# Long cross attention: a fourth PSUM bank for the maxima, and the jobs beside the loop in the banks of the scores

## The reference, cut to what matters

```
q = x @ Wq            # (8, 100, 16 heads, 8)
k = context @ Wk      # (8, 1444, 4 heads, 8)
v = context @ Wv
s = q . k / sqrt(8)   # each query head against its group's key head
a = softmax(s over the 1444 keys)
x = x + (a @ v) @ Wo
```

## Time and profile before

| | |
|---|---|
| median of three runs | 1079.68 us |
| the profiled execution | 1077.89 us, span 1076.1 us |
| loop of maxima | 811.7 to 1037.6 us |
| one full pass (six in a row alike) | 28.65 us |
| busy in such a pass | PE 26.8, DVE 25.7, ACT 22.2, POOL 4.1 us |
| granted TensorE clock in it | 1.00 |

### The profile page before, as it was taken

One profiled execution on the slowest core, in us unless ns is written; L12 is line 12 of the kernel. 1 busy time (PEld: TensorE's weight loads), 2 busy tenths in 40 slices (PEclk: granted clock), 3 DMA queues, 4 the chain that ended last, 5 costly groups with the idle time before them and its releaser, 6 DMA issues. The chain is left out here.

```text
span 1076.1 us, 18489 instructions
## 1 busy us (share of the span) xinstructions
PE 894.8 (83%) x6288; PEld 549.2 (51%) x6294; DVE 740.2 (69%) x2034; ACT 583.9 (54%) x1772; POOL 243.5 (23%) x357
## 2 busy tenths in 40 slices
PE   6998999999798273499669799795768999999997
PEld 3346999999465131345443486482752233333333
DVE  7568778777575599376777555514558888988953
ACT  5785777777433100243535344641443777777784
POOL 5004455555200122133030000351401111111110
PEclk9699999999999586599888899996885999999999
DMA  9600000000002700100001002550202001111000
GB/s 232 160 22 1 2 2 2 1 2 2 1 1 35 88 0 2 29 2 1 1 25 32 1 1 71 171 147 16 53 16 63 20 12 24 28 28 21 2 1 16
DMA packets 76185, 35.83 MB, mean 33 GB/s; under 512 B 35236, under 2 KB 74571, under 8 KB 76092
## 3 DMA queue, kind: packets, MB, share of 16 engines
q1 hardware_dynamic: 73724, 33.61, 14.0%
q0 software_dynamic: 896, 0.63, 0.2%
q10 hardware_dynamic: 1472, 0.41, 0.2%
HBM read 24.42 MB, written 11.05 MB: 33 GB/s over the span
## 5 line engine op out<-in xcount | busy, mean ns | idle before, releaser
L503 DVE TENSOR_REDUCE L3x_NMP<-L3x_pM 128x1 f32<-128x361 f32 x384 | 178.2, 525 | 19.9 <-PE L3x_pM L736 19.1
L657 ACT ACTIVATE L3x_E<-L3x_pS 128x400 f32<-128x400 f32 (+1 forms) x375 | 164.5, 509 | 47.2 <-PE L3x_pS L760 46.1
L736 PE MATMUL L3x_pM<-ctx_tm 64*128 64x361 bf16 x384 | 103.7, 340 | 13.9 <-DVE L3x_NMP L503 9.5
L760 PE MATMUL L3x_pS<-ctx_tm 64*128 64x400 bf16 (+1 forms) x375 | 105.4, 350 | 1.6 <-POOL ctx_tm L447 1.2
L1869 ACT ACTIVATE L0x_E<-L0x_E,ctx_r 128x100 f32<-128x100 f32 x288 | 105.1, 369 | 0.5 <-DVE L0x_E L1749 0.5
L736 PEld LDWEIGHTS L3x_pM<-ctx_tm 64*128 64x128 bf16 x384 | 30.2, 96 | 109.4 <-DVE L3x_NMP L503 90.4
L777 PE MATMUL L3x_pO<-L3x_E,CT 128*32 128x400 f32 (+1 forms) x768 | 85.1, 515 | 0.6 <-ACT L3x_E L657 0.4
L1678 POOL TENSOR_TENSOR L0x_E<-L0x_E,L0x_RZ 128x1200 f32<-128x1200 f32 x24 | 52.6, 2194 | 72.3 <-DVE L0x_RZ L1774 72.3
L1995 PE MATMUL L0x_pU<-ctx_tm,L0x_E 128*100 128x129 f32 x576 | 67.8, 273 | 1.1 <-POOL L0x_E L1678 1.1
L1983 PE MATMUL L0x_pS<-L0x_QS,CT 128*128 128x100 f32 x576 | 68.4, 275 | 0.0
L1983 PEld LDWEIGHTS L0x_pS<-L0x_QS,CT 128*128 128x128 f32 x576 | 66.2, 192 | 0.4 <-ACT L0x_QS L1861 0.4
(11 more groups left out here) (706 smaller groups left out, 2122.3 us busy)
## 6 DMA issues: line engine op xcount, KB each, us to landing
ctx_tm<-in_ctx SPq DMA_DIRECT2D x8, 704.0 KB
ctx_tm<-key_terms SPq DMA_DIRECT2D x16, 270.8 KB, 4.2
key_terms<-ctx_tm SPq DMA_DIRECT2D x42, 90.2 KB
ctx_tm<-in_L_ffn_wi SPq DMA_DIRECT2D x4, 512.0 KB, 8.0
ctx_tm<-in_L_ffn_wo SPq DMA_DIRECT2D x4, 512.0 KB, 8.1
ctx_tm<-query_terms SPq DMA_DIRECT2D x16, 75.0 KB, 3.5
slots_in<-L2a_zeros SPq DMA_DIRECT2D x8, 129.0 KB
L2f_XS<-slots_in SPq DMA_DIRECT2D x4, 258.0 KB, 3.4
```

The source lines that it names most:

```text
L503: nc.vector.tensor_reduce(NMP[:, p, i // NC4, a, i % NC4:i % NC4 + 1], v, AX.X, ALU.max, negate=True).then_inc(s_mr, 1)
L657: nc.scalar.activation(E[0:r, n % EB, :], score_bank(n)[0:r, 0:NG * T], ACT.Exp, scale=SCALE8).then_inc(s_e, 1)
L736: nc.tensor.matmul(pM[:, n % 3, 0:CW], key_rows(QS, a)[:, b, p, 128 * x:128 * x + 128], key_rows(KS, a)[:, b % KB, c, p, :], start=True, s ...
L760: nc.tensor.matmul(score_bank(n)[0:NW[k], 0:NG * T], key_rows(KS, a)[:, b % KB, k % 4, p, 128 * (k // 4):128 * (k // 4) + NW[k]], key_rows ...
```

## The change

`pP` goes, and its bank becomes the fourth of `pM`; product n for the maxima now goes to bank n mod 4 and waits for the reduction four before it. The jobs have no bank of their own any more. A loop that runs when the program is built (`banks_in_turn`) goes through the steps and gives each score product and each job one of the three banks of `pS`, always the one that it counts free first. It counts a score's bank free 1 or 1.4 steps after its step, and a job's after the number of steps in `JOB_READ`. It also notes who held the bank before; TensorE waits for the reader of that holder, with `s_e` if it was a score, with `s_read` if it was a job. From the last unit on two banks of `pM` are used as well, and once the maxima are through (t of 208 and more) the jobs go to the fourth bank of `pM`.

```diff
-        pM = s.ps("pM", [128, 3, 512])
+        pM = s.ps("pM", [128, 4, 512])
         pS = s.ps("pS", [128, 3, 512])
         pO = s.ps("pO", [128, 512])
-        pP = s.ps("pP", [128, 512])
...
-        def score_bank(n):
-            return job_banks[n % 3 if n < MORE else (n - MORE) % 5]
...
+        JOB_READ = {"NT": 1.8, "TM": 4.8, "TURN": 1.8, "PROJ": 1.4}
+        shared = [pS[:, 0, :], pS[:, 1, :], pS[:, 2, :], pM[:, 1, :], pM[:, 2, :]]
+        def banks_in_turn():
+            bank, earlier = {}, {}
+            free, holder = [0.0] * len(shared), [None] * len(shared)
+            def take(item, t, until):
+                usable = 5 if t >= start(NU - 1) else 3
+                i = min(range(usable), key=lambda x: free[x])
+                bank[item], earlier[item] = shared[i], holder[i]
+                free[i], holder[i] = until, item
+            for t in range(LAST + 1):
+                at_step = unit_step(t)
+                if at_step is not None:
+                    for a in range(2):
+                        take(("score", 24 * at_step[0] + 2 * at_step[1] + a), t, t + 1 + 0.4 * a)
+                for job in jobs_at(t):
+                    if t >= DRAIN:
+                        bank[job] = pM[:, 3, :]
+                    else:
+                        take(job, t, t + JOB_READ[job[0]])
+            return bank, earlier
...
+                def bank_read(item):
+                    holder = earlier_in_bank[item]
+                    if holder is not None and holder[0] == "score":
+                        pe.wait_ge(s_e, holder[1] + 1)
+                    elif holder is not None:
+                        pe.wait_ge(s_read, number[holder] + 1)
...
-                    if n >= 3:
-                        pe.wait_ge(s_mr, n - 2)
+                    if n >= 4:
+                        pe.wait_ge(s_mr, n - 3)
...
-                    if n >= 3 and bank_reader(n):
-                        pe.wait_ge(s_e, bank_reader(n))
-                    elif n >= 3:
+                    bank_read(("score", n))
+                    if n >= 24 * (NU - 1):
                         pe.wait_ge(s_mr, 2 * DRAIN)
```

More of the change, by code:

```diff
@@ L250, in attention_long @@
     DRAIN = PER * B
-    MORE = 24 * (NU - 1)
     IT = 4
@@ L307, in attention_long @@
         pT = [pS[:, 2, :], pO]
-        job_banks = [pS[:, i, :] for i in range(3)] + [pM[:, 1, :], pM[:, 2, :]]
-        def score_bank(n):
-            return job_banks[n % 3 if n < MORE else (n - MORE) % 5]
[L313 to L317, removed]
         def start(u):
@@ L362, in attention_long, with score_bank @@
                 number[job] = len(number)
+        JOB_READ = {"NT": 1.8, "TM": 4.8, "TURN": 1.8, "PROJ": 1.4}
[19 more added lines that the diff above has]
+            return bank, earlier
+        bank_of, earlier_in_bank = banks_in_turn()
+        def score_bank(n):
+            return bank_of["score", n]
         def key_rows(ap, a):
@@ L494, in maximum @@
                     dve.wait_ge(s_m, m_count(n + 1))
-                    v = pM[:, n % 3, 0:CW]
+                    v = pM[:, n % 4, 0:CW]
                     if o // 2 in (REM_AT, REM_AT + 1):
@@ L522, in normalised @@
                         dve.wait_ge(s_fill, number["TURN", b - 1] + 1)
+                    pP = bank_of["TM", b]
                     chain.then(nc.vector.reciprocal(rden[:, :], pP[0:T, D:D + NH]))
@@ L530, in residual @@
                     dve.wait_ge(s_fill, number["PROJ", b] + 1)
-                    nc.vector.tensor_tensor(m.X[:, b, :], m.X[:, b, :], pP[0:T, 256:256 + D], ALU.add)\
+                    nc.vector.tensor_tensor(m.X[:, b, :], m.X[:, b, :], bank_of["PROJ", b][0:T, 256:256 + D],
+                                            ALU.add)\
                       .then_inc(s_read, 1)
@@ L669, in maxima @@
                         act.wait_ge(s_add, u - 1)
-                    nc.scalar.copy(NB[:, u % 2, :], pP[:, 0:NG * T]).then_inc(s_read, 1)
+                    nc.scalar.copy(NB[:, u % 2, :], bank_of["NT", u][:, 0:NG * T]).then_inc(s_read, 1)
                 def outT(b):
@@ L675, in outT @@
                         act.wait_ge(s_fill, number["PROJ", b - 1] + 1)
-                    nc.scalar.copy(OT[:, :], pP[:, 144:144 + T]).then_inc(s_read, 1)
+                    nc.scalar.copy(OT[:, :], bank_of["TURN", b][:, 144:144 + T]).then_inc(s_read, 1)
                 for t in range(LAST + 1):
@@ L706, in fill @@
                         pe.wait_ge(s_read, number[job])
+                    if job in earlier_in_bank:
+                        bank_read(job)
+                    else:
+                        pe.wait_ge(s_mr, 2 * DRAIN)
+                    return bank_of[job]
                 for i, (a, e) in enumerate(PARTS):
@@ L729, in max_scores @@
                         for p in range(2):
-                            nc.tensor.matmul(pM[32 * p:32 * p + 32, n % 3, 0:CW], QR[:, p, b, :],
+                            nc.tensor.matmul(pM[32 * p:32 * p + 32, n % 4, 0:CW], QR[:, p, b, :],
                                              KS[:, b % KB, c, p, :], start=True, stop=True,
@@ L740, in turn_maxima @@
                 def turn_maxima(u):
-                    fill(("NT", u))
+                    pP = fill(("NT", u))
                     pe.wait_ge(s_mx, u + 1)
@@ L794, in turn @@
                 def turn(b):
-                    fill(("TURN", b))
+                    pP = fill(("TURN", b))
                     nc.tensor.transpose(pP[:, 144:144 + T], ON[:, :], m.ident[0:T, 0:T]).then_inc(s_fill, 1)
                 def project(b):
-                    fill(("PROJ", b))
+                    pP = fill(("PROJ", b))
                     nc.tensor.matmul(pP[0:T, 256:256 + D], OT[:, :], wo[:, :], start=True, stop=True)\
```

2 lines of the change are left out of this document (1 added, 1 removed).

## The result

The changed kernel is slower. Its median of four runs is 1097.28 us (1093.19 to 1102.62), beside 1079.30 us (1077.50 to 1080.97) for four runs of the kernel before. The ratio is 1.0165, with a 95% interval of 1.0139 to 1.0190. The profiled execution took 1093.19 us, the lowest of the four, with a span of 1091.4 us. The forecast of 1089 us had the sign right and was 8 us short; the result lies 4 us above the forecast's own range (1083 to 1093) and 3 us above the wider one (1076 to 1094).

A forecast was written before the change was run, and what follows sets the result against it. VectorE bounds, sometimes starved by TensorE's late products. Head -2.45, six passes +12.4 and the end +0.2 give some +10.2 on the profiled 1077.89, 1088.1, or 1089.9 by median; forecast 1089, range 1083 to 1093, wider 1076 to 1094.

The forecast's parts named there:

- The walk: Event-by-event count through pass 3 with unit costs, each engine in written order: pass 30.8 us, 2.1 longer than 28.65.
- the score of step 18: TensorE there since 3.0, score waits for ScalarE's copy of NT until 4.40; the deciding wait, found as 1.4 us.
- that of step 1: Score waits for VectorE's division of TM, going at 14.93 where TensorE stood since 13.4; reduction 56 at 16.52, before 15.45.
- that of step 9: Second score waits for the residual behind reduction 71, ending at 25.52; VectorE's queue empties, reduction 72 at 26.11, before 23.67.
- NT goes at 1.45: Step 16: bank's exponential done at 1.34, GpSimd's split at 1.39, so NT goes at 1.45; reduction 34 at 3.0 against 3.32.
- zero: Start of reduction 28 in the walked pass 3 (910.59 in the profile before); the walk's times count from it.
- VectorE-bound, 4.69 us against 4.98: Last stretch of a pass, from reduction 72 to the next zero: VectorE-bound, 4.69 us against 4.98 before.
- The first pass: Pass of 27.95 us, partly at 1.2 GHz: idle gaps -1.0, plain waits -1.9, one job +0.9.
- the third: Rival, starved passes: late weighted sums delay exponentials and copies, every event 0.2 worse, +3.5 a pass, 1097; chance 0.07.
- The second, the fourth bank wins: Rival: readers' waits fall into the 0.81 us of slack, pass 26.4 or 27, total 1064; chance 0.14.
- The rule: Repeated gaps on the engine that should be saturated suggest lacking PSUM, use all eight banks; alone it implied 1064.
- The first, near balance: Rival: readers' waits real, two-bank stretches and steps around TM cost nothing, about 0 a pass, 1075 to 1081; chance 0.13.

The follow-up runs named there:

- the residual alone moved: Changed kernel with only VectorE's addition of PROJ moved ahead of the two reductions of step 9: 1087.36 us, a full pass 30.41 us.
- the longer claim: Changed kernel with only larger JOB_READ numbers (NT 2.9, TM 5.9, PROJ 3.9 steps), readers not moved: 1085.40 us, ratio 1.0016 to the kernel before.
- the filling: Changed kernel with eight useless products for the maxima ahead of the score that waits for PROJ's reader: 1094.92 us, ratio 1.0141 to the kernel before.
- the division's: Changed kernel with only VectorE's division of TM moved ahead of the two reductions of step 0: 1092.34 us, a full pass 30.31 us.
- the copy's kernels: Changed kernel with only ScalarE's copies of NT moved ahead of its exponentials of steps 17 and 3: 1089.15 us, a full pass 30.13 us.
- the sharing alone: Changed kernel with three banks for the maxima again, jobs still in the scores' banks, eighth bank only in the tail: 1108.89 us, ratio 1.0239.

## Why the prediction was right in sign and short in size

**The sign, and where it is decided: right.** The walk named the score of step 18 behind the copy, that of step 1 behind the division and that of step 9 behind the residual. They are the three waits of TensorE, and undoing each saves 0.9 to 1.2 us. At step 18 both ends came later than in the walk: TensorE stands there from 3.62 and not 3.0, and the score goes at 4.71 and not 4.40, so the wait is 1.09 us for the 1.4 of the prediction. VectorE's waits rose above 16.0 us, most of them in lumps of 0.5 to 0.8. They are not fewer, as I had it, but 57 for 54.

**"NT goes at 1.45": the step that failed first.** I took the exponential that frees `NT`'s bank to end at 1.34. It is the second of the four that start 0.79 behind zero, as they did before; it ends at 1.69, and `NT` went at 1.79. The fourth bank did not bring these exponentials forward: the weighted sum of step 14 stands ahead of their scores, and it starts 0.43 ahead of zero (912.98) as it did before. So at step 16 the bank gave nothing, not even for a moment, and everything behind is late by as much. Against the walk, in us behind zero:

| reduction | before | walk | measured |
|---|---|---|---|
| 34 | 3.32 | 3.00 | 3.33 |
| 38 | 5.40 | 5.99 | 6.34 |
| 52 | 13.19 | 13.41 | 13.65 |
| 56 | 15.45 | 16.52 | 16.76 |
| 64 | 19.58 | 21.69 | 21.94 |
| 72 | 23.67 | 26.11 | 26.34 |
| next zero | 28.65 | 30.80 | 31.30 |

From reduction 34 to 72 the walk is right to 0.12 us: it lost 0.33 at its first step and was 0.23 off at the end.

**"VectorE-bound, 4.69 us against 4.98": the second.** From reduction 72 to the next zero took 4.96. VectorE waits at step 13, 0.34 us in pass 3, where the walk had it busy throughout:

```profile
943.22 1.05 DVE L516 TENSOR_REDUCE L3x_NRP<-L3x_pM 64x1 f32<-64x361 f32 x2 [0.34 <-PE L3x_pM L762]
```

The walk had TensorE held at step 9 until VectorE's queue was empty, and then let VectorE run as if products were in store for it again. They are not. Where TensorE is held at step 9 for less, the walk's figure is nearly right: with the residual alone moved, on the same banks, TensorE waits there for 0.5 us, VectorE's wait at step 13 is gone from all six passes, and the stretch takes 4.75 us. With the longer claim, where TensorE does not wait for the residual at all, it takes 4.75 as well. The same four reductions of steps 12 and 13 with the residual moved:

```profile
940.42 2.15 DVE L516 TENSOR_REDUCE L3x_NRP<-L3x_pM 64x1 f32<-64x361 f32 x4
```

So the fourth bank does help here, but not behind the residual's wait. The miss is 0.27 us a pass. The two steps together are 0.5 a pass and 3.0 us in six; another 0.3 is the 2.15 that I had rounded to 2.1.

**The clock: not in the sum.** 2.9 us in two passes. The walk had the wait at step 9, and treated a wait as costing its own length.

**The first pass: right by luck.** Predicted 2.0 shorter, measured 1.9. But the profile with the filling, whose first pass is the same program, has 27.12 us for it, with the clock up from the 1.2 GHz level 11.7 us behind zero, where it is 8.5 us in the changed kernel's and 11.6 in the one of before. A window of each at the change of the clock, first the changed kernel's, then that with the filling:

```profile
831.45:832.45 1.00, 1.00 (x10) 0.11 (x4) 0.89 (x3) 0.24 (x1) 0.00 (x0) 0.73 0.06 16
```

```profile
835.21:836.21 1.00, 1.00 (x10) 0.04 (x4) 0.81 (x4) 0.37 (x1) 0.07 (x1) 0.65 0.00 0
```

So 27.95 - 27.12 = 0.8 is what banks and order give, and 1.1 is when the clock came up. Why it comes up earlier in some executions stays open.

**The sum.** Predicted +10.2, of it +12.4 for six passes. Measured +18.6 for these: 3.3 more for the walk and 2.9 for the clock. Set against that, 1.45 us came from a stage that started earlier, and a start like that moves without any change: the second profile of the changed kernel starts its first pass 4.7 us later than the first one, and from there to the end both take 267.9 us, where the kernel before takes 250.8. That is 17.1 us. Both profiles of the changed kernel have the early clock in the first pass, though, so with the 1.1 us for it the change costs some 18.2; the medians differ by 18.0.

**The rivals.** The result is near the 1097 of the third, but its mechanism is not there: lateness does not grow from event to event. The second, the fourth bank wins, took the bank to be worth 3.4 us a pass; with the jobs in the scores' banks it is worth 1.1. The rule that I had set beside it (the Trainium skill, Perfetto Trace Analysis, Optimization Strategy) reads such repeated gaps as a possible lack of PSUM. The trace agreed on the gaps, but not that one more bank would cover each, as I had written: by my own working a fourth bank covers 0.44 us of lateness more, and the wait of 0.60 at reduction 34 is longer and stayed. The runs add that a bank taken from a side job cost 3.8 where it gave 1.1. The first, near balance, is where the kernel with a longer claim comes out: 1.0016.

## What to carry to other kernels

When buffers are shared by a static table, a buffer's lifetime ends where its reader stands in its engine's queue, and not where its data are ready: moving the readers ahead of work that could wait turned +1.7% into -0.4%. In such a walk take a release from the row of the instruction that gives it; do not let it move forward because of the change before you have checked what else holds it. Do not count a bank's slack again right behind a wait that has used it up. And give a new wait of 1.4 us on TensorE a price beyond its length, since here the clock fell behind it in a third of the cases.

## What the runs showed of the hardware

- In stretches where TensorE is otherwise at 2.4 GHz, a single wait of 1.39 us was followed by some 3.4 us at 1.2 GHz in 7 of the 20 passes that have one (the changed kernel twice, the division's and the copy's kernels), at a price of 1.44 to 1.53 us each. The changed kernel's waits of 0.99, 1.09 and 1.24 us were followed by no fall. With the sharing alone there was one long fall, of 6.8 us, in a pass that was 2.1 us longer; it began 2.1 us behind the 1.09 us at step 18 and inside a further wait of 0.46 us, so the residual's wait is not the only one that can bring it.
- It falls in the same passes (2 and 5) in both profiles of the changed kernel, though their stages began 4.7 us apart.
- 1.4 us of products that nobody reads, in place of the wait, went with a clock of 1.00 in all six passes of one profile, where the score still came no earlier.
- The first pass runs its first 8.4 to 8.7 us at 1.2 GHz in seven of the fourteen profiles and its first 11.3 to 12.0 us in the other seven. The same program had 8.5 in two profiles and 11.7 in one, which moves that pass by 1.1 us.
